# A linear-attention and expert kernel: every second unit of scaled q turned by a transposing DMA, units taken in pairs

## The reference, cut to what matters

```python
q = relu(ln(x) @ Wq)              # x: 2048 x 512, Wq: 512 x 2048, 32 heads of 64
k = relu(ln(x) @ Wk); v = ln(x) @ Wv
kv = einsum('bhsd,bhse->bhde', k, v)
normalizer = clip(einsum('bhsd,bhd->bhs', q, k.sum(axis=2)), 1e-06)
x = x + (einsum('bhsd,bhde->bhse', q, kv) / normalizer) @ Wo + bo
# then, on ln(x): scores of 8 experts, the best two, silu(x @ w1.T + b1) @ w2.T + b2, weighted sum, added to x
```

## Time and profile before

| | us |
|---|---|
| median of 3 runs | 992.87 (992.55 to 995.8) |
| the profiled execution | 993.69 |
| its span, first to last instruction | 992.0 |
| PE busy | 979.3 (99%) |
| DVE, ACT, POOL busy | 714.3, 553.7, 248.5 |

### The profile page before, as it was taken

How to read it: one execution, slowest core, us unless ns; L and a number is a source line. 1 busy time by engine, 2 the same in 40 slices (tenths; PEclk the granted TensorE clock), 3 DMA queues, 4 the chain that set the end, 5 groups by cost and what they waited for, 6 DMA issues and landing times.

```text
span 992.0 us, 17230 instructions
## 1 busy us (share of the span) xinstructions
PE 979.3 (99%) x4863; PEld 823.5 (83%) x4863; DVE 714.3 (72%) x1594; ACT 553.7 (56%) x1376; POOL 248.5 (25%) x407
## 2 busy tenths in 40 slices
PE   9999999999999999999999999999999999999997
PEld 7888888888888888888788888888888888888896
DVE  7888665665656676757878787888887786677674
ACT  5445544444445445865556556655555796565553
POOL 1000000000000002221644343444443573433334
PEclk9999999999999999999999999999999999999999
DMA  7012654555555531333221111111114765787773
GB/s 267 4 40 86 212 170 170 170 184 187 188 188 190 188 122 64 107 123 96 86 72 57 53 53 53 53 53 60 56 43 138 230 195 95 119 115 110 119 114 49
DMA packets 121048, 116.15 MB, mean 117 GB/s; under 512 B 47049, under 2 KB 95354, under 8 KB 120866
## 3 DMA queue, kind: packets, MB, share of 16 engines
q1 hardware_dynamic: 111746, 98.51, 32.7%
q0 software_dynamic: 9248, 16.95, 9.1%
HBM read 42.91 MB, written 64.14 MB: 108 GB/s over the span
## 4 chain that ended last, share of the span: by engine, by line
PE 89%; DVE 4%; ACT 3%; DMA 2%; issue 1%; POOL 0%; POOLq 0%; ACTq 0%; DVEq 0%; SPq 0%
PE pK L1739 13%; PE pK L1741 13%; PE pK L1740 13%; PE pA L1739 8%; PE pA L1741 8%; PE pA L1740 8%; PE pX L1739 5%; PE pX L1741 5%; PE pX L1740 5%; PE pA L1873 3%; DMA out<-y,slot_token 2%; PE pT L1819 2%; ACT w_hi L1152 1%; PE pX L2108 1%; PE pT L1754 1%
## 5 line engine op out<-in xcount | busy, mean ns | idle before, releaser
L1006 ACT ACTIVATE qs<-q,nrec 128x64 f32<-128x64 f32 x512 | 129.6, 335 | 88.3 <-DVE nrec L1437 88.2
L622 POOL TENSOR_TENSOR wv_lo<-wv_in,wv_hi 128x512 fp32r<-128x512 f32 x4 | 5.2, 1298 | 403.2 <-ACT wo_hi L927 403.2
L1739 PE MATMUL pA<-k_hi,xn_hi 128*128 128x512 f32 x256 | 101.0, 394 | 0.5 <-DVE k_lo L1312 0.5
L1739 PE MATMUL pK<-wq_hi,xnT_hi 128*128 128x512 f32 x256 | 100.4, 392 | 0.0
L1739 PE MATMUL pK<-wk_hi,xnT_hi 128*128 128x512 f32 (+1 forms) x256 | 100.0, 391 | 0.1
L1741 PE MATMUL pK<-wq_hi,xnT_lo 128*128 128x512 f32 x256 | 99.9, 390 | 0.0
L1741 PE MATMUL pA<-k_hi,xn_lo 128*128 128x512 f32 x256 | 99.8, 390 | 0.0
L1740 PE MATMUL pK<-wk_lo,xnT_hi 128*128 128x512 f32 (+1 forms) x256 | 99.8, 390 | 0.0
L1740 PE MATMUL pK<-wq_lo,xnT_hi 128*128 128x512 f32 x256 | 99.7, 389 | 0.0
L1740 PE MATMUL pA<-k_lo,xn_hi 128*128 128x512 f32 x256 | 99.7, 389 | 0.0
L1741 PE MATMUL pK<-wk_hi,xnT_lo 128*128 128x512 f32 (+1 forms) x256 | 99.6, 389 | 0.0
(11 more groups left out here) (302 smaller groups left out, 2457.3 us busy)
## 6 DMA issues: line engine op xcount, KB each, us to landing
xr_dram<-zero SPq DMA_DIRECT2D x10, 3584.0 KB, 12.8
w_in<-in_ffn_w SPq DMA_DIRECT2D x22, 256.0 KB, 4.0
w_in<-in_ffn_w SPq DMA_DIRECT2D x8, 704.0 KB, 6.5
xn<-in_attn_hidden_states SPq DMA_DIRECT2D x16, 256.0 KB, 5.6
wv_in<-in_attn_Wv SPq DMA_DIRECT2D x16, 256.0 KB, 2.8
wo_in<-in_attn_Wo SPq DMA_DIRECT2D x16, 256.0 KB, 3.0
wk_in<-in_attn_Wq SPq DMA_DIRECT2D x4, 1024.0 KB, 5.7
xnT_dram<-xnT SPq DMA_DIRECT2D x4, 1024.0 KB, 11.7
```

The lines of the kernel that those rows point to most:

```text
L1006: i = nc.scalar.activation(qs[:, s], q[:, s], ACT.Copy, scale=nrec[:, b * HC + h:b * HC + h + 1])
L1739: nc.tensor.matmul(dst, lhs[0], rhs[0], start=start, stop=False)
```

## The change

From unit 15 to unit 61 every odd unit (24 of them) is not turned by PE. ACT writes the low and high halves of its words as two planes of 16 bits (`put_qs_planes`, 128x1024) into `qs_planes`, SP issues a transposing DMA into `qsT_planes` (`turn_qs`), ACT and DVE each write one plane back as words into the odd half of `qs` (`join_low`, `join_high`), ACT takes the high part from there (`act_joined`) and DVE the low part (`dve_joined`). `qs_planes` lies over the odd half of `q`, and `qsT_planes` over the odd half of `qsT_lo`. Even units and unit 63 are turned by PE as before.

From tile 4 the units go in pairs. For m even, PE does `project_q(m)`, `project_q(m + 1)`, `times_m(m - 2)`, `times_m(m - 1)`, `transpose_qs(m)`; ACT and DVE follow in the order that the diff shows.

```diff
+    qs_planes = sb("qs_planes", 2 * CW, 146 * KB, U16)
+    qsT_planes = sb("qsT_planes", 2 * CW, 142 * KB, U16)
...
+            def turn_qs(m, nth):
+                sp.wait_ge(qs_planes_ready, nth)
+                sp.wait_ge(o_put, m - 1)
+                sp.dma_start_transpose(qsT_planes[:, :].rearrange("p (c n) -> p c n", n=P), qs_planes[:, :]).then_inc(s_qsT, 16)
...
-            def tile_io(t):
+            def tile_io(t, turning=False):
                 if not (isinstance(t, int) and t == 1):
                     next_xnT(t)
+                if turning:
+                    turn_qs(4 * t + 1, turned(1, t))
...
-            with sp.Fori(3, NT - 2) as t:
-                tile_io(t)
-            tile_io(NT - 2)
+            tile_io(3)
+            turn_qs(15, 1)
+            for t in range(4, NT - 2):
+                tile_io(t, True)
+                turn_qs(4 * t + 3, turned(2, t))
...
+            def put_qs_planes(m):
+                act.wait_ge(qs_ready, m + 1)
+                nc.scalar.copy(planes(qs_planes), words(qs[:, CW:2 * CW])).then_inc(qs_planes_ready, 1)
+
+            def join_low(nth):
+                act.wait_ge(s_qsT, 16 * nth)
+                nc.scalar.copy(qsT_words(0), planes(qsT_planes)[:, 0, :]).then_inc(qs_low_joined, 1)
+
+            def act_joined(m, nth):
+                act.wait_ge(qs_low_joined, nth)
+                act.wait_ge(qs_high_joined, nth)
+                act.wait_ge(o_put, m - 1)
+                nc.scalar.copy(qsT_hi[:, CW:2 * CW], qs[:, CW:2 * CW]).then_inc(qsT_hi_ready, 1)
...
             def act_tile(t, b):
-                for c in range(NC):
-                    m = 4 * t + c
-                    act_q(m, c % 2)
-                    if c == 0 and not (isinstance(t, int) and t == NT - 1):
+                for p in range(2):
+                    m = 4 * t + 2 * p
+                    act_q(m, 0)
+                    if p == 0 and not (isinstance(t, int) and t == NT - 1):
                         act_qx(t + 1, 1 - b)
-                    act_qsT(m - 1, (c - 1) % 2)
-                    if c == 2:
+                    join_low(turned(p, t))
+                    act_joined(m - 1, turned(p, t))
+                    if p == 1:
                         sqrt_var(NT + t - 1)
-                    act_qs(m, c % 2)
-                    if c == 1:
+                    act_q(m + 1, 1)
+                    act_qs(m, 0)
+                    act_qs(m + 1, 1)
+                    if not (isinstance(t, int) and t == NT - 1 and p == 1):
+                        put_qs_planes(m + 1)
+                    act_qsT(m, 0, 2 * t + (8 + p))
+                    if p == 0:
                         put_planes(t - 2)
...
+            def join_high(nth):
+                dve.wait_ge(s_qsT, 16 * nth)
+                nc.vector.tensor_copy(qsT_words(1), planes(qsT_planes)[:, 1, :]).then_inc(qs_high_joined, 1)
+
+            def dve_joined(m):
+                dve.wait_ge(qsT_hi_ready, m + 1)
+                lo(qsT_lo[:, CW:2 * CW], qs[:, CW:2 * CW], qsT_hi[:, CW:2 * CW]).then_inc(qsT_lo_ready, 1)
...
             def dve_tile(t, b):
+                for p in range(2):
+                    m = 4 * t + 2 * p
+                    join_high(turned(p, t))
+                    dve_q(m, 2 * p, 0, 2 * t + (7 + p))
+                    dve_joined(m - 1)
+                    if p == 0 and not (isinstance(t, int) and t == NT - 1):
+                        dve_qx(t + 1, 1 - b)
+                    if p == 1:
+                        put_slot8(t - 2, b)
+                    dve_q(m + 1, 2 * p + 1, 1)
+                    if p == 0:
+                        dots(t - 2, 4, E)
+                        put_scores(t - 2)
                         x2_stats(t - 1)
+                    else:
                         layernorm2(t - 1)
                         dots(t - 1, 0, 4)
+                    dve_qsT(m, 0)
...
             def pe_tile(t, b):
+                for p in range(2):
+                    m = 4 * t + 2 * p
+                    project_q(m, t, 2 * p, b)
+                    project_q(m + 1, t, 2 * p + 1, b)
+                    if p == 1:
+                        rank(t - 2, b)
                         pe.wait_ge(x2_ready, t)
+                    times_m(m - 2, (2 * p - 2) % 4, 0, pX[:, :])
+                    times_m(m - 1, (2 * p - 1) % 4, 1, pX[:, :])
+                    transpose_qs(m, 0)
...
+            transpose_qs(4 * NT - 1, 1)
             w_transpose(0)
             w_transpose(1)
-            transpose_qs(4 * NT - 1, 1)
             times_m(4 * NT - 2, 2, 0, pX[:, :])
```

More of the change, by code:

```diff
@@ L309, in block_kernel @@
         qsT_put = sem("qsT_put")
+        qs_planes_ready = sem("qs_planes_ready")
+        s_qsT = sem("s_qsT")
+        qs_low_joined = sem("qs_low_joined")
+        qs_high_joined = sem("qs_high_joined")
         qsT_hi_ready = sem("qsT_hi_ready")
@@ L423, in block_kernel @@
         planes = lambda a: a[:, :].rearrange("p (h n) -> p h n", h=2)
+        turned = lambda p, t: 2 * t - 7 + p
+        qsT_words = lambda h: qs[:, CW:2 * CW].bitcast(U16).rearrange("p (n h) -> p h n", h=2)[:, h, :]
         words = lambda a: a.bitcast(U16).rearrange("p (n h) -> p h n", h=2)
@@ L536, in _ @@
             load_w1(4, 6, s_w1a)
-            with sp.Fori(3, NT - 2) as t:
-                tile_io(t)
-            tile_io(NT - 2)
+            tile_io(3)
[3 more added lines that the diff above has]
+                turn_qs(4 * t + 3, turned(2, t))
+            tile_io(NT - 2, True)
+            turn_qs(4 * NT - 5, turned(2, NT - 2))
+            turn_qs(4 * NT - 3, turned(1, NT - 1))
             def load_w2(e):
@@ L1007, in act_qs, with act_qsT @@
                 i.then_inc(qs_ready, 1)
-            def act_qsT(m, b):
-                act.wait_ge(qsT_put, m + 1)
+            def act_qsT(m, b, put=None):
+                act.wait_ge(qsT_put, m + 1 if put is None else put)
                 if not (isinstance(m, int) and m < 2):
@@ L1125, in _ @@
             act_unit(15, 3)
+            put_qs_planes(15)
             def act_tile(t, b):
-                for c in range(NC):
-                    m = 4 * t + c
-                    act_q(m, c % 2)
-                    if c == 0 and not (isinstance(t, int) and t == NT - 1):
+                for p in range(2):
+                    m = 4 * t + 2 * p
+                    act_q(m, 0)
+                    if p == 0 and not (isinstance(t, int) and t == NT - 1):
                         act_qx(t + 1, 1 - b)
-                    act_qsT(m - 1, (c - 1) % 2)
-                    if c == 2:
+                    join_low(turned(p, t))
+                    act_joined(m - 1, turned(p, t))
+                    if p == 1:
                         sqrt_var(NT + t - 1)
-                    act_qs(m, c % 2)
-                    if c == 1:
+                    act_q(m + 1, 1)
[5 more added lines that the diff above has]
+                    if p == 0:
                         put_planes(t - 2)
@@ L1144, in _ @@
             act_tile(NT - 1, 1)
-            act_qsT(4 * NT - 1, 1)
+            act_qsT(4 * NT - 1, 1, 2 * NT + 8)
             put_planes(NT - 2)
@@ L1424, in _, with dve_q @@
             heads = lambda a: a.rearrange("p (h d) -> p h d", h=HC)
-            def dve_q(m, c, b):
-                if not (isinstance(m, int) and m < 2):
+            def dve_q(m, c, b, put=None):
+                if put is not None:
+                    dve.wait_ge(qsT_put, put)
+                elif not isinstance(m, int) or m > 16:
+                    dve.wait_ge(qsT_lo_ready, m - 1)
+                elif m > 1:
                     dve.wait_ge(qsT_put, m - 1)
@@ L1585, in dve_tile @@
             def dve_tile(t, b):
-                for c in range(NC):
-                    m = 4 * t + c
-                    if c == 2:
-                        x2_stats(t - 1)
[L1590 to L1598, removed]
+                for p in range(2):
[11 more added lines that the diff above has]
+                        put_scores(t - 2)
+                        x2_stats(t - 1)
+                    else:
                         layernorm2(t - 1)
-                    if c == 3:
-                        put_slot8(t - 2, b)
                         dots(t - 1, 0, 4)
+                    dve_qsT(m, 0)
             with dve.Fori(2, NT // 2 - 1) as h:
@@ L1972, in pe_tile @@
             def pe_tile(t, b):
[L1973 to L1977, removed]
+                for p in range(2):
[4 more added lines that the diff above has]
+                        rank(t - 2, b)
                         pe.wait_ge(x2_ready, t)
-                    if c == 3:
-                        rank(t - 2, b)
-                    times_m(m - 2, (c - 2) % 4, c % 2, pX[:, :])
+                    times_m(m - 2, (2 * p - 2) % 4, 0, pX[:, :])
+                    times_m(m - 1, (2 * p - 1) % 4, 1, pX[:, :])
+                    transpose_qs(m, 0)
             for c in range(NC):
```

## The result

| | before | after |
|---|---|---|
| median of six runs each, us | 992.71 (992.05 to 995.8) | 998.12 (997.2 to 998.87) |
| ratio to before, 95% interval | | 1.0052 [1.0042, 1.0063] |
| the profiled execution, us (span) | 993.69 (992.0) | 997.85 (996.1) |

The change makes the kernel 5.4 us slower, 0.5%, with an interval that leaves out 1. The forecast was 984, faster by 9; the time lies inside the range to 1004, on the side of the rival that was given 0.25.

The account below looks back on a forecast made before the run. PE was taken to bound the kernel. The profiled 993.69 us, less 10.6 for removed transposes, plus 1.5 at the ends, gave 984.6; the median, 0.8 lower, was forecast as 984 us, range 981.5 to 1004.

Parts of the forecast that it names:

- L: Time from issue to landing of the transposing DMA; taken as 2.9 us, with ends of 2.0 and 5.6.
- the ends: Extra waiting at the kernel's start (0.5 us) and end (1 us); together 1.5 us, between 0 and 3.
- break-even: Loop length per pair at which the change gains nothing: 11.91 us, reached at L = 3.5 us.
- Removed: Four PE transposes of 0.44 us together, gone from each of 24 odd units: 10.6 us saved.
- Pairs cost PE nothing: Ordering PE's units in pairs from tile 4 was claimed to cost PE nothing by itself.
- The loop of 8.4 us plus L: One landing to the next, through DVE's joins and sums, ACT's scalings and planes, and SP's issue: 8.4 us plus L.
- Few collisions with xb: DVE sums slowed beside POOL's xb were expected to be few; one in each tile would be 1.1 us.
- The threshold: PE stays the bound while the loop per pair is under 11.47 us, that is L under 3.1 us.
- one rival of 984 to 989 us: Loop a little too long, from L of 3.1 to 3.3 or xb collisions; chance 0.17, shared with DVE as bound.
- the landing is late: L over 3.5 us at DVE's join_high and ACT's join_low; 1006 us at L = 4, 1044 at 5.6; chance 0.25.
- What would show it: Signs in the profile: tiles of 22.9 to 23.0 us; PE waiting for qsT_lo in each pair would prove it wrong.

Follow-up runs that it names:

- e10: Changed kernel with row scatters held until the second pair's landing and POOL's xb cut to 8 of 512 columns from tile 4; 986.35 us, ratio 0.9921.
- e6: Changed kernel's order in pairs, but PE turns every unit, without planes, joins or transposing DMAs; 993.19 us, ratio 0.9999 to the kernel before.
- e3: Changed kernel, but from tile 4 POOL's xb addition covers only 8 of 512 columns; 988.17 us, ratio 0.9921 to the kernel before.
- e9: Changed kernel, but in tiles 4 to 13 POOL's row scatters wait until the second pair's transposing DMA has landed; 991.62 us, ratio 0.9978.
- e5: Changed kernel with join_high behind the even unit's dve_q, next x's low part before dve_joined, unit 62's low part ahead of the dots; 988.19 us, ratio 0.9952.
- e11: e5 with the row scatters held until after the landing, as in e9; 987.04 us, ratio 0.9932 to the kernel before.
- e7: Changed kernel, but SP first copies the planes by a plain DMA and waits for it before the transposing one; 1049.0 us, ratio 1.0556.
- e8: e5 with the extra plain DMA of e7 ahead of the transposing one; 1032.34 us, ratio 1.0389 to the kernel before.

## Why the prediction was wrong

The prediction gave a gain of 9 us and the kernel lost 5.4. It was right in mechanism, the loop against PE, and failed in the sizes of three terms: L, the join beside xb, and the ends. With the first two at their measured sizes its own loop is over the break-even.

- **Removed: 10.6 us.** Held. The middle tile of e10 is 23.79 - 22.80 = 0.99 us shorter (0.88 forecast), and its Q 8.8 us shorter, against 10.6 - 1.5 = 9.1 forecast with the ends. The second agreement is partly luck: the tiles gain more and the start costs more than forecast.
- **Pairs cost PE nothing.** Held (e6).
- **The loop of 8.4 us plus L.** The links were right and their sum a little high: 8.32 us in the first stretch (12.10 - 3.78), 8.82 in the second, 7.9 of it without the slow join; mean 8.1.
- **L = 2.9 us.** This failed. It is 3.05 us undisturbed, which both of my nearest rows had missed by only 0.15, and 3.8 for the DMA of every second pair, beside the scatters; mean 3.43. I had named the scatters, and then argued them away by the DMA share of 0.18. A mean over a tile says nothing about the microsecond in which two transfers meet.
- **Few collisions with xb.** This failed too. I had counted on xb falling while DVE waits for the landing. It fell on the landing itself, 0.03 to 0.42 us ahead of the join, and so once in each of 12 tiles. The likely reason is that both follow from the same pair of PE and keep their distance; that was not tried by itself. The price was about right: 1.42 - 0.47 = 0.95 us a tile, where 1.1 was given. The number of collisions was not.
- **The threshold.** PE stays the bound under 11.47 us, and the break-even is 11.91 for a pair. Measured: 11.98. Either disturbance alone leaves a gain (e3 clearly, e9 by 0.2%); only both together make it a loss. I had counted them as alternatives within one rival of 984 to 989 us, and never added L of 3.4 and a slow join: 8.4 + 3.4 + 0.45 = 12.25, which is on the slower side. The rival "the landing is late" had the right sign, but its condition, L over 3.5 us, was met in one landing of two only; the mean of 3.43 without the slow joins would have left a gain, as e3 shows.
- **The ends: 1.5 us.** This failed as well. Measured are waits of 2.33 at the start and, at the end, 0.98 and 0.48 (PE for a scaled q at 777.17), 3.8 us in all, and behind the first of them 1.4 us at the lower clock (last section); 3 was my upper end. The end's part is gone in e10, so it came from the loop being late; the start's 2.4 is there in e10 too, and was counted as 0.5. The chain of the changed kernel shows what I left out there: the sums of unit 15 meet POOL, and 1.5 us are lost on the way to the first landing. The kernel before has the same slow instruction (2.21 us at 485.28), and PE waits only 0.80 us soon after it (490.84).

```profile
484.37 2.20 DVE qs L1475
```

- **What would show it.** "The prediction is wrong if PE waits for `qsT_lo` in each pair" was the right sign: its weight loads do, 23 times.

The rule in "VectorE: DVE Perf Modes", section Rules for kernel authors, of the Trainium skill, to transpose 128x128 on TensorE where PSUM will do, came out right in sign for this kernel, and not by the figure in its section The three transpose paths: an estimate from its 1309 ns a block would be 10.5 us for eight blocks, and the landing is 3.05. e5 shows the other way round with the same DMA.

## What to carry to other kernels

When a change puts a DMA's landing into a loop across engines, write down the loop's sum and compare it with the bound, as here, but then add all known disturbances at once, since a margin of 0.2 us in 11.5 is none. Put the wait behind the work that doesn't need it, and fill the gap that this opens on the next engine; here that turned 0.5% slower into 0.5% faster with the same instructions. A collision in a steady loop came in each tile, not now and then: look at the distance of the two instructions, not at how rarely they could meet.

## What the runs showed of the hardware

A 16-bit copy of 128x512 on DVE, SBUF to SBUF, with a single input, takes 0.47 us alone and 1.20 to 1.58 beside POOL's addition of 1.29 us. That it is held until POOL is done can be read from the rows: POOL ends at 577.89 + 1.29 = 579.18, the copy at 579.50; in the slowest and the fastest of the 12 the copy also ends 0.32 us behind POOL. It goes the other way too. In e11 a DVE instruction with two SBUF inputs starts 0.04 us ahead, and POOL is the one that takes 0.5 us longer. The row of POOL, and the row of DVE:

```profile
574.14 1.80 POOL L662 TENSOR_TENSOR xb<-x_in,bo_b 128x512 f32<-128x512 f32 x1 [0.29 <-POOL vals L713]
```

```profile
574.10 0.68 DVE L1482 TENSOR_TENSOR qs<-q,ksum 128x512 f32<-128x512 f32 x1
```

By "SBUF — State Buffer", section SBUF: two separate sides, of the Trainium skill, whichever of the two takes the shared port pair first holds it for its whole instruction and the other blocks; the rows here agree in both directions. The row at 484.37 above is less simple: the DVE instruction starts 0.34 us ahead of xb (484.71), and still it is the one that is held, to 0.56 us behind xb's end. A scatter of POOL, `meta_dram`, was under way when it started (483.72, 0.96 us), which may be what held it first; no run tried that.

A transposing DMA of 256 KB from SBUF to SBUF: issue 1.24 us, landing 3.05 us alone and 3.8 beside two row scatters. A plain one: issue 0.47, landing 2.26 alone and 2.88 beside them (e7). The 0.79 us between the landings is the 0.77 between the issues. "Advanced Engine Details and Errata", X-Bar Transpose (TRN2), of the Trainium skill has transposing DMAs as fast as plain ones; for the latency of a single one of this size the rows don't agree.

What an idle PE costs beyond the idle time was unexpected. In e8, PE's last matmul before a wait is at 580.43, and it goes on at 583.18. Then the chain reads:

```profile
583.91 0.23 PE pX L1801
...
584.55 0.43 PE pX L1800
```

And by stretches (length, busy us of PE, PEld, DVE, ACT, POOL, then the granted clock, DMA share, GB/s):

```profile
580.00:583.10 3.10, 0.82 (x4) 0.35 (x2) 1.69 (x3) 2.08 (x5) 0.00 (x0) 1.00 0.03 7
584.00:587.50 3.50, 3.50 (x10) 2.74 (x9) 3.43 (x11) 3.13 (x13) 0.00 (x0) 0.51 0.05 18
```

After the wait of 2.37 us the granted clock is 0.51 from 584.0 to 587.5, the 1.2 GHz level, and a matmul takes 0.43 us instead of 0.23; from 587.5 on it is 1.00 again. Eight matmuls at 0.2 us more are 1.6 us of PE's time, which is more than half of the wait again. In e8 most of it is hidden, because the loop is the bound: the next join starts 0.39 us behind its landing (594.01 against 593.62), and the chain shows no other delay from it in that tile. The changed kernel does the same once, behind its wait of 2.33 us at the start:

```profile
497.50:500.50 3.00, 3.00 (x9) 2.31 (x7) 2.88 (x9) 2.10 (x10) 0.20 (x1) 0.50 0.53 81
```

There PE is the bound, and seven matmuls at 0.2 us more, 1.4 us, come on top of the wait. The waits of the middle tiles, 0.6 us at most, did nothing of the kind: the clock from 510 to 750 us reads 1.00.
